# A gather, combine and scatter stage: ten groups of 500 edges in place of twenty pairs of 128

## The chip, the cores and the metric

The kernel runs on one core of a Trainium2 chip. The metric is the device time of one execution in microseconds. The engines are PE (matrix products), DVE (vector), ACT (scalar), POOL (which also issues the indirect DMAs) and SP (which issues plain DMAs); each works through its own queue in order, and they wait for one another by semaphores.

## What is computed

A graph layer with its normalizations, followed by a small mixture of experts. The change touches the graph layer's edge stage alone:

```python
x = layernorm(x)                                  # 10000 x 512
msg = relu(x[src] + edge_attr @ W_e + b_e)        # 5000 edges, 64 attributes each
aggr = segment_sum(msg, dst, num_segments=10000)  # dst is sorted, with many repeats
h = (1 + eps) * x + aggr
h = silu(batchnorm(h @ W1 + b1)); h = silu(batchnorm(h @ W2 + b2))
x = x0 + h                                        # x0 as it was; then the experts
```

## The kernel before

Four stages run one after the other, `edge_aggregate`, `gnn_up`, `gnn_down` and `mixture`; each ends when all its engines are done. Between the first two lies the table `aggregate` in the chip's memory, 10,000 rows of 512 numbers and some rows more for what is thrown away. SP fills it with zeros in pieces of 1 MB (L161), the edge stage adds the messages to it by indirect DMAs that add at the destination (`scatter`, L263), and `gnn_up` reads it.

The 5000 edges go in 20 pairs of tiles of 128 edges, the last one padded. Four sets of buffers (`PU`) are used in turn. For a pair g:

- SP (ACT for the first four) loads source and destination indices by column, the attributes, and the destinations by row, repeated over all partitions (`load`, L136, seven DMAs).
- POOL gathers 2 x 128 rows of `x` by source index into `xg` (`gather`, L248).
- DVE's `front` (L293) compares each destination with all destinations of the pair, which gives the 0/1 matrix `sel` (L304). With `before` it finds out whether an edge has an earlier one with the same destination (L309); the address `idx` of such an edge is a row that is thrown away (L319). Then the mean and the variance of each gathered row (L315 to L326).
- POOL's `root` (L257) takes the inverse root, DVE's `shift` the bias (L329).
- PE's `embed` (L367) transposes the attributes and multiplies them by `web`, in float32. ACT's `normalize` (L192) makes `xn`, DVE's `add` (L335) adds the product from PSUM, ACT takes the positive part `msg` (L212).
- PE's `combine` (L381) multiplies `msg` by `sel` in float32, so that every edge holds the sum of all edges of the pair with its destination; ACT copies that from PSUM to `comb` (L220).
- POOL scatters the 2 x 128 rows. Since two pairs can hold the same destination, each scatter waits until the one before it has landed (semaphore `sca`, L266).

The order of POOL's queue is: for each pair scatter(g), gather(g+4), root(g+3). DVE's: shift(g+1), add(g), front(g+2). ACT's: attributes(g+1), the positive part of g, normalize(g+1), the copy of g. Two turns before the end DVE also splits W1 into a high and a low part (L406 to L409), for the products of the next stage.

Of the kernel before, what the change touches and what calls it, by code (L numbers as in the profile page):

```python
# [14 lines left out]
P = 128  # L15
# [4 lines left out]
PAIRS = -(-E // (2 * P))  # L20
ER = E - (PAIRS * 2 - 1) * P
PU = 4
ROOTS = 3
ZQ = 3
TRASH = 2 * P
# [25 lines left out]
def edge_aggregate(nc, sem, psum, ident, x, src, dst, edge_attr, W_e, b_e, agg, W1, w1, vectors, vec):  # L51
# [5 lines left out]
    with ExitStack() as ctx:  # L57
        def sb(name, shape, dt=F32):
            return ctx.enter_context(nc.sbuf_tensor(name, shape, dt))

        def buffers(name, shape, dt=F32, n=PU):
            return [sb(f"{name}{i}", shape, dt) for i in range(n)]

        zeros = sb("zeros", [P, 2048])
        web = sb("web", [ED + 1, H])
        before = sb("before", [P, 2, 2 * P])
        trash = sb("trash", [P, 2])
        mhalf = sb("mhalf_e", [P, 2])
        eaT = sb("eaT", [ED + 1, PU, 2 * P])


        dcol, scol = buffers("dcol", [P, 2], I32, PU + 1), buffers("scol", [P, 2], I32, PU + 1)
        drow, ea = buffers("drow", [P, 2 * P], I32, PU + 1), buffers("ea", [P, 2, ED], F32, PU + 1)
        xg = buffers("xg", [P, 2, H])
        dcolf, cnt, away = buffers("dcolf", [P, 2]), buffers("cnt", [P, 2]), buffers("away", [P, 2])
        sel, scr = buffers("sel", [P, 2, 2 * P]), sb("scr", [P, 2, 2 * P])
        idx = buffers("idx", [P, 2], I32)
        st, mv = buffers("est", [P, 2, 6]), buffers("emv", [P, 2, 2])
        ve, rs, nb = buffers("eve", [P, 2]), buffers("ers", [P, 2]), buffers("enb", [P, 2])
        xn, pre = buffers("exn", [P, 2, H]), buffers("pre", [P, 2, H])  # L80
        msg, comb = buffers("msg", [P, 2, H]), buffers("comb", [P, 2, H])
        tp, emb, cps = psum[0:2], psum[2:6], psum[6:8]
# [3 lines left out]
        vld = sem("vectors_loaded")  # L86
        w1ld, w1h, w1l = sem("w1_loaded"), sem("w1_hi_done"), sem("w1_lo_done")
        ld = [sem(f"edge_loaded{i}") for i in range(PU + 1)]
        gat = [sem(f"rows_gathered{i}") for i in range(PU)]
        sca = sem("rows_added")  # L90
        dcf, sl, ct, aw, ix = sem("dstf"), sem("sel_ready"), sem("cnt_ready"), sem("away_ready"), sem("idx_ready")
        bst, bag, vpe, rst, nbr = sem("estats"), sem("emeanvar"), sem("evar_eps"), sem("erstd"), sem("emean_rstd")
        xnr, prr, msr = sem("exn_ready"), sem("pre_ready"), sem("msg_ready")
        tpr, etr, emr, cpr, cbr = sem("ea_transposed"), sem("eaT_ready"), sem("emb_ready"), sem("comb_psum"), sem("comb_ready")
        CONST = 10
        LOADS = 7 * 16
# [3 lines left out]
        pieces = [(c, min(c + 2048, cols)) for c in range(0, cols, 2048)]  # L100
        TURNS = PAIRS // PU

        def pair_of(it, u):

            it, u = it + u // PU, u % PU
            return it * PU + u, u, it

        def inputs(g, u):

            return PU if isinstance(g, int) and g == PAIRS - 1 else u  # L110

        def loaded(g, u, it):

            return (ld[PU], LOADS) if inputs(g, u) == PU else (ld[u], (it + 1) * LOADS)

        def turns(eng, turn):

            turn(0)
            with eng.Fori(1, TURNS - 2) as it:
                turn(it)  # L120
            turn(TURNS - 2)
            turn(TURNS - 1)

        def exists(it, u):

            return not isinstance(it, int) or it * PU + u < PAIRS

        def from_(g, least):

            return not isinstance(g, int) or g >= least  # L130

        def all_zero(eng):
            for i in range(ZQ):
                eng.wait_ge(zeroed[i], 16 * len(pieces[i::ZQ]))

        def load(eng, it, u):  # L136
            g, u, it = pair_of(it, u)
            i, e0 = inputs(g, u), g * 2 * P
            if i == u and from_(g, PU):

                wait_apart(eng, (const, CONST), (ix, 2 * (g - PU + 1)), (gat[u], it * 32), (tpr, g - PU + 1))
            rows = (P, P) if i == u else (P, ER)
            for j, p in enumerate(rows):
                span = bass.ds(e0 + j * P, p)
                eng.dma_start(scol[i][0:p, j:j + 1], src[span].rearrange("(p a) -> p a", a=1)).then_inc(ld[i], 16)
                eng.dma_start(dcol[i][0:p, j:j + 1], dst[span].rearrange("(p a) -> p a", a=1)).then_inc(ld[i], 16)
                eng.dma_start(ea[i][0:p, j, :], edge_attr[span, :]).then_inc(ld[i], 16)
            eng.dma_start(drow[i][:, 0:sum(rows)], dst[bass.ds(e0, sum(rows))].rearrange("(a p) -> a p", a=1)
                          .to_broadcast([P, sum(rows)])).then_inc(ld[i], 16)

        with nc.Block() as block:
            @block.sync
            def _(sp):
                sp.dma_start(web[0:ED, :], W_e).then_inc(wld, 16)
                sp.dma_start(web[ED:ED + 1, :], b_e.rearrange("(a n) -> a n", a=1)).then_inc(wld, 16)

                sp.wait_ge(const, 1)
                for i, (c0, c1) in enumerate(pieces):
                    if i >= ZQ:
# [1369 lines left out]
```

## Time and profile before

| | us |
|---|---|
| three runs, median (lowest to highest) | 2173.71 (2170.03 to 2175.91) |
| the profiled execution | 2172.88 |
| its span | 2171.1 |
| edge stage, first instruction to the next stage's first load | 2.2 to 242.4 |

| engine | busy us of the span | share |
|---|---|---|
| PE | 1948.6 | 90% |
| DVE | 1212.7 | 56% |
| ACT | 1005.5 | 46% |
| POOL | 387.8 | 18% |

A share of the whole span is a mean over four stages; for the edge stage one reads the views cut to its stretch of time. Timelines give an operation's start and length, and in brackets how long its engine had nothing to do before it, and what ended that.

### The profile page before, as it was taken

The numbers are of one execution on the slowest core, as the hardware profiler recorded it, in microseconds if no ns is written. First come the engines' busy times: TensorE is split into PE (matmuls) and PEld (weight loads), VectorE is DVE, ScalarE is ACT, GpSimd is POOL, SyncE is SP. The second block draws the span as 40 slices with busy tenths as digits, with TensorE's granted clock in tenths as the row PEclk, the third lists the DMA queues.
The fourth block names the chain that finished last, engine by engine and source line by source line (L and its number), as shares of the span: only waits on it lengthen the run. The fifth ranks groups of instructions, "written<-read, shape, count | busy, mean of one in ns | idle before, by whom it ended". The sixth has DMA issues, their size and how long they took to land. (4 is left out here: it accounts for less than half of the span.)

```text
span 2171.1 us, 42529 instructions
## 1 busy us (share of the span) xinstructions
PE 1948.6 (90%) x15080; PEld 1395.1 (64%) x15080; DVE 1212.7 (56%) x2533; ACT 1005.5 (46%) x1742; POOL 387.8 (18%) x481
## 2 busy tenths in 40 slices
PE   0777399999999799999999589999899999999997
PEld 0233278888888588888887466656666666666653
DVE  1457356566566343434342667667576676767654
ACT  0445123333233375656563455546464554655542
POOL 1576230000000000000000422212121221222200
PEclk9999699999999899999999799999999999999999
DMA  9886746566656443434341744334343333434311
GB/s 379 205 153 122 161 132 184 158 180 182 166 169 171 151 152 118 165 118 165 117 166 56 242 152 137 105 103 131 95 128 99 127 112 100 136 104 137 99 55 64
DMA packets 182828, 309.29 MB, mean 142 GB/s; under 512 B 33065, under 2 KB 107305, under 8 KB 179594
## 3 DMA queue, kind: packets, MB, share of 16 engines
q1 hardware_dynamic: 169674, 285.35, 42.0%
q0 software_dynamic: 8960, 20.98, 5.1%
q8 instruction: 103, 1.69, 0.3%
q10 hardware_dynamic: 4032, 0.80, 0.2%
q14 instruction: 59, 0.48, 0.1%
HBM read 172.20 MB, written 134.87 MB: 141 GB/s over the span
## 5 line engine op out<-in xcount | busy, mean ns | idle before, releaser
L1397 PE MATMUL bank<-f2s,inner_bd 128*32 128x512 f32 x2560 | 304.8, 606 | 1.5 <-issue 1.2
L1301 ACT ACTIVATE inter_hi<-bank 128x512 fp32r<-128x512 f32 x320 | 191.2, 598 | 200.3 <-PE bank L1397 199.4
L1232 DVE TENSOR_TENSOR inter_lo<-bank,inter_hi 128x512 fp32r<-128x512 f32 x320 | 220.1, 689 | 95.7 <-ACT inter_hi L1301 95.0
L419 PE MATMUL bank<-ahi,w_hi 128*128 128x500 f32 x640 | 250.8, 392 | 14.4 <-DVE alo L760 14.4
L606 ACT ACTIVATE h1o<-bank,b_by_channel 128x500 f32<-128x500 f32 x160 | 108.5, 678 | 327.4 <-PE bank L421 327.4
L419 PE MATMUL bank<-hhi,w_hi 128*128 128x500 f32 x640 | 251.6, 393 | 2.5 <-DVE hlo L567 2.5
L421 PE MATMUL bank<-hhi,w_lo 128*128 128x500 f32 x640 | 249.8, 390 | 0.0
L420 PE MATMUL bank<-hlo,w_hi 128*128 128x500 f32 x640 | 249.4, 390 | 0.0
L420 PE MATMUL bank<-alo,w_hi 128*128 128x500 f32 x640 | 249.2, 389 | 0.0
L421 PE MATMUL bank<-ahi,w_lo 128*128 128x500 f32 x640 | 248.9, 389 | 0.0
L1281 ACT ACTIVATE yT<-bank 128x512 f32<-128x512 f32 x320 | 173.6, 597 | 83.8 <-PE bank L1371 83.2
L573 DVE BATCH_NORM_STATS2 stats<-h1o 128x500 f32 (+1 forms) x160 | 103.6, 676 | 163.0 <-ACT h1o L606 163.0
L1397 PEld LDWEIGHTS bank<-f2s,inner_bd 128*32 128x32 f32 x2560 | 74.1, 111 | 148.0 <-issue 145.5
L760 DVE TENSOR_TENSOR alo<-a_whole,ahi 128x500 fp32r<-128x500 f32 x160 | 108.7, 679 | 106.3 <-ACT ahi L796 106.3
L766 DVE BATCH_NORM_STATS2 stats<-h2o 128x500 f32 (+1 forms) x80 | 52.6, 677 | 175.5 <-ACT h2o L804 175.5
L419 PEld LDWEIGHTS bank<-ahi,w_hi 128*128 128x128 f32 x640 | 120.6, 189 | 42.1 <-DVE alo L760 17.8
L1370 PE MATMUL bank<-perm_bd,xn_hi 128*128 128x512 f32 x320 | 140.9, 440 | 2.2 <-ACT yT L1281 2.2
L419 PEld LDWEIGHTS bank<-hhi,w_hi 128*128 128x128 f32 x640 | 120.7, 189 | 26.8 <-DVE hlo L567 2.9
L1406 PE MATMUL bank<-inter_hi,back_bd 128*128 128x512 f32 x320 | 128.1, 400 | 10.2 <-DVE back_bd L1224 10.2
L421 PEld LDWEIGHTS bank<-hhi,w_lo 128*128 128x128 f32 x640 | 120.9, 189 | 24.9
L421 PEld LDWEIGHTS bank<-ahi,w_lo 128*128 128x128 f32 x640 | 120.7, 189 | 25.1
L420 PEld LDWEIGHTS bank<-hlo,w_hi 128*128 128x128 f32 x640 | 120.9, 189 | 24.6
(124 smaller groups left out, 3287.1 us busy)
## 6 DMA issues: line engine op xcount, KB each, us to landing
h1T<-h1o SPq DMA_DIRECT2D x19, 2000.0 KB, 8.1
h1in<-h1T SPq DMA_DIRECT2D x19, 2000.0 KB, 9.6
aggregate<-zeros SPq DMA_DIRECT2D x20, 1024.0 KB, 8.3
h2in<-h2T SPq DMA_DIRECT2D x40, 512.0 KB, 4.0
x<-in_x SPq DMA_DIRECT2D x80, 256.0 KB, 2.6
x<-x SPq DMA_DIRECT2D x80, 256.0 KB, 3.8
x_back<-x SPq DMA_DIRECT2D x80, 256.0 KB, 3.8
out<-x_back SPq DMA_DIRECT2D x80, 256.0 KB, 2.0
```

The costliest lines, as they stand in the source:

```text
L419: nc.tensor.matmul(out, w_hi[:, k, cols], a_hi[:, k, :], start=(k == 0), stop=False)
L420: nc.tensor.matmul(out, w_hi[:, k, cols], a_lo[:, k, :], start=False, stop=False)
L421: last = nc.tensor.matmul(out, w_lo[:, k, cols], a_hi[:, k, :], start=False, stop=(k == chunks - 1))
L573: nc.vector.bn_stats(stats1[:, m, bass.ds(c * 6, 6)], h1o[b][:, m, :]).then_inc(str_, 1)
L606: nc.scalar.activation(h1o[b][:, m, :], mb[m % 4][:, 0:CW], ACT.Identity, bias=b1c[:, m:m + 1]).then_inc(evr, 1)
L760: nc.vector.tensor_tensor(alo[b][:, k, :], aw[:, k, :], ahi[b][:, k, :].bitcast(F32), ALU.subtract).then_inc(lor, 1)
L1232: nc.vector.tensor_tensor(ilo[u % QB][:, :], bI[u % QB][:, :], ihi[u % QB][:, :].bitcast(F32), ALU.subtract).then_inc(ilr, 1)
L1281: nc.scalar.activation(yT[:, c, :, j * GB:(j + 1) * GB], bD[c % 2][:, :].rearrange("p (e g) -> p e g", g=GB), ACT.Copy).then_inc(yr, 1)
L1301: nc.scalar.activation(ihi[n % QB][:, :], bI[n % QB][:, :], ACT.Copy).then_inc(ihr, 1)
L1370: nc.tensor.matmul(o, xhi[j % 2][:, c * P:(c + 1) * P], r, start=True, stop=False)
L1397: last = nc.tensor.matmul(bI[b][32 * i:32 * i + 32, :], ibd[:, e, j, :, :].rearrange("p s g -> p (s g)"), f2s[:, e, :], start=True, stop=True)
L1406: nc.tensor.matmul(bA[:, :], rbd[:, b, :], ihi[b][:, :], start=(b == 0), stop=False)
```

## The change

The edges go in ten windows of four tiles of 125 edges. Edge number p x 40 + t stands in row p of tile t, so that one DMA loads all source indices, one all destinations and two all attributes, ahead of the zeros. Gathers and scatters still move 128 rows per tile; the last three are padding (source 0, destination a row that is thrown away, three rows of zeros in `comb`).

- Destinations by row come from PE (`spread`: a transpose of the repeated column, into one bank of PSUM), no longer from a DMA. DVE compares straight from that bank.
- A window's tiles share destinations, so tile j of a window sums over tiles j to 3 of it: ten products with a `sel` of 125 x 125. They are made twice, for a high and a low part of the message, in float32r (`mhi`, `mlo`, which lie in the buffers of W2).
- ACT's `normalize` is gone. DVE makes x times the inverse deviation plus the embedding in one instruction, ACT adds the bias with the positive part, and copies that to the high part; DVE subtracts it for the low part.
- Four windows of gathered rows (`XW`) are kept, two windows of `comb`.
- W1 and the vectors are loaded after the zeros. W1 is split at the end of DVE's queue.
- All loops are written out, with no loop in the hardware.

In the diff below the bodies of `matches`, `statistics` and `attributes`, the declarations and the constants' set-up are left out.

```diff
-PAIRS = -(-E // (2 * P))
-PU = 4
-ROOTS = 3
-TRASH = 2 * P
+EP, ET = 125, 40
+EW = 4
+EN = ET // EW
+XW = 4
+TRASH = EW * P
...
@@ SP @@
+                sp.dma_start(scol[0:EP, :], src.rearrange("(p i) -> p i", i=ET)).then_inc(lds, 16)
+                sp.dma_start(dcol[0:EP, :], dst.rearrange("(p i) -> p i", i=ET)).then_inc(ldd, 16)
+                attr = edge_attr.rearrange("(p i) d -> p i d", i=ET)
+                for p0, p1 in ((0, EP // 16 * 16), (EP // 16 * 16, EP)):
+                    sp.dma_start(ea[p0:p1, :, :], attr[p0:p1]).then_inc(lde, 16)
...
@@ ACT @@
+                def messages(w):
+
+                    for t in window(w):
+                        s = slot(t)
+                        act.wait_ge(prr, t + 1)
+                        nc.scalar.activation(xg[0:EP, s, :], xg[0:EP, s, :], ACT.Relu, bias=nb[0:EP, t:t + 1]).then_inc(msr, 1)
+                        act.wait_ge(msr, t + 1)
+                        if w >= 2:
+                            act.wait_ge(cpr, EW * (w - 1))
+                        nc.scalar.activation(mhi[0:EP, t % (2 * EW), :], xg[0:EP, s, :], ACT.Copy).then_inc(mhr, 1)
+
+                def collect(w):
+
+                    if w >= 2:
+                        act.wait_ge(sca, 16 * EW * (w - 1))
+                    for t in window(w):
+                        act.wait_ge(cpr, t + 1)
+                        nc.scalar.activation(comb[0:EP, t % (2 * EW), :], cps[t % 3][0:EP, :], ACT.Copy).then_inc(cbr, 1)
+
+                for w in range(EN):
+                    if w + 1 < EN:
+                        attributes(w + 1)
+                    messages(w)
+                    if w >= 1:
+                        collect(w - 1)
+                collect(EN - 1)
...
@@ POOL @@
+                def gather(w):
+                    if w >= XW:
+
+                        pool.wait_ge(mhr, EW * (w - XW + 1))
+                        pool.wait_ge(mlr, EW * (w - XW + 1))
+                    for t in window(w):
                         nc.gpsimd.indirect_dma_start(
+                            out=xg[:, slot(t), :], out_offset=None, in_=x, in_offset=bass.IndirectOffsetOnAxis(
+                                ap=scol[:, t:t + 1], axis=0)).then_inc(gat[w % XW], 16)
+                def scatter(w):
+
+                    pool.wait_ge(ix, w + 1)
+                    if w >= 1:
+                        pool.wait_ge(sca, 16 * EW * w)
+                    for t in window(w):
+                        pool.wait_ge(cbr, t + 1)
                         nc.gpsimd.indirect_dma_start(
...
+                for w in range(XW):
+                    gather(w)
+                for w in range(XW - 1):
+                    root(w)
+                for i in range(ZQ):
+                    pool.wait_ge(zeroed[i], 16 * len(pieces[i::ZQ]))
+                for w in range(EN):
+                    scatter(w)
+                    if w + XW < EN:
+                        gather(w + XW)
+                    if w + XW - 1 < EN:
+                        root(w + XW - 1)
...
@@ DVE @@
+                def combine(w):
+
+                    a, b = w * EW, (w + 1) * EW
+                    dve.wait_ge(rst, w + 1)
+                    nc.vector.scalar_tensor_tensor(out=nb[0:EP, a:b], in0=mv[0:EP, a:b, 0], scalar=-1.0, in1=rs[0:EP, a:b],
...
+                    for t in window(w):
+                        dve.wait_ge(emr, t + 1)
+                        nc.vector.scalar_tensor_tensor(out=xg[0:EP, slot(t), :], in0=xg[0:EP, slot(t), :],
+                                                       scalar=rs[0:EP, t:t + 1], in1=emb[t % 2][0:EP, :],
+                                                       op0=ALU.mult, op1=ALU.add).then_inc(prr, 1)
+                    if w >= 2:
+                        dve.wait_ge(cpr, EW * (w - 1))
+                    for t in window(w):
+                        dve.wait_ge(mhr, t + 1)
+                        nc.vector.tensor_tensor(mlo[0:EP, t % (2 * EW), :], xg[0:EP, slot(t), :],
+                                                mhi[0:EP, t % (2 * EW), :].bitcast(F32), ALU.subtract).then_inc(mlr, 1)
+
+                matches(0)
+                statistics(0)
+                statistics(1)
+                for w in range(EN):
+                    if w + 1 < EN:
+                        matches(w + 1)
+                    if w + 2 < EN:
+                        statistics(w + 2)
+                    combine(w)
+                dve.wait_ge(w1ld, 16)
+                for k in range(KH):
+                    split_weight(nc.vector, w1["whole"], w1["hi"], w1["lo"], w1h, w1l, k)
...
@@ PE @@
+                def embed(w):
+                    pe.wait_ge(etr, w + 1)
+                    for t in window(w):
+                        j = t % EW
+                        if t >= 2:
+                            pe.wait_ge(prr, t - 1)
+                        nc.tensor.matmul(emb[t % 2][0:EP, :], eaT[:, w % 2, j * EP:(j + 1) * EP], web[:, :],
                                          start=True, stop=True).then_inc(emr, 1)
...
+                def add_up(w):
+                    pe.wait_ge(mlr, EW * (w + 1))
+                    for t in window(w):
+                        j = t % EW
+                        if t >= 3:
+                            pe.wait_ge(cbr, t - 2)
+                        for i in range(j, EW):
+                            s = (w % 2) * EW + i
+                            pick = sel[w % 3][i][0:EP, j * EP:(j + 1) * EP]
+                            nc.tensor.matmul(cps[t % 3][0:EP, :], pick, mhi[0:EP, s, :], start=(i == j), stop=False)
+                            last = nc.tensor.matmul(cps[t % 3][0:EP, :], pick, mlo[0:EP, s, :], start=False,
+                                                    stop=(i == EW - 1))
...
+                for w in range(EN):
+                    if w + 1 < EN:
+                        spread(w + 1)
+                        turn(w + 1)
+                    embed(w)
+                    if w >= 1:
+                        add_up(w - 1)
+                add_up(EN - 1)
```

`matches(w)` compares tile i with tiles 0 to i of its window (125 to 500 columns), finds earlier edges of the same destination with `before`, and makes `idx`; it waits for `spread(w)`, which in turn waits until the comparisons of the window before have read the bank. `statistics(w)` waits for all four gathers of the window. `turn` transposes the attributes.

## Rows read from the trace of the kernel before

**Rows 1.** Busy time by stage: span, busy us (instructions) by engine, clock, DMA share, GB/s.
```profile
68.00:236.00 168.00, 120.60 (x257) 48.15 (x255) 89.91 (x315) 74.33 (x128) 111.84 (x89) 0.89 0.76 141
```

**Rows 2.** Waits, 60 to 240 us: who waited for whom, total us, times, longest.
```profile
POOL aggregate L269 <- DMA aggregate<-comb,idx: 31.4, 14, 5.8
```

**Rows 3.** Timeline of POOL: start us, us, operation, [idle before <- what ended it].
```profile
115.37 1.64 POOL L269 DMA_INDIRECT aggregate<-comb,idx  x1 [1.22 <-DMA aggregate<-comb,idx]
...
117.31 1.57 POOL L269 DMA_INDIRECT aggregate<-comb,idx  x1 [0.30 <-ACT exn L199]
...
119.19 1.02 POOL L253 DMA_INDIRECT xg<-in_x,scol  x1 [0.30 <-issue]
...
120.52 0.98 POOL L253 DMA_INDIRECT xg<-in_x,scol  x1 [0.30 <-issue]
...
123.22 1.64 POOL L269 DMA_INDIRECT aggregate<-comb,idx  x1 [0.97 <-ACT comb L220]
```

**Rows 4.** DVE's groups up to 240 us (busy, mean ns), and its timeline from 249.
```profile
L343 DVE TENSOR_TENSOR pre<-exn,bank 128x512 f32<-128x512 f32 x40 | 25.8, 684 | 2.4 <-ACT exn L199 1.9
...
L309 DVE CUSTOM_DVE_ANT_0 scr<-sel,before 128x256 f32<-128x256 f32 x40 | 15.2, 416 | 0.0
...
L409 DVE TENSOR_TENSOR w_lo<-weight_whole,w_hi 128x1024 fp32r<-128x1024 f32 x4 | 4.9, 1226 | 0.1
...
249.46 2.47 DVE L543 BATCH_NORM_STATS2 st<-xt 125x6 f32<-125x512 f32 x4 [6.84 <-DMA xt<-in_x]
...
252.26 0.17 DVE L548 TENSOR_SCALAR ve<-mv 125x4 f32<-125x4 f32 x1
```

**Rows 5.** ACT's groups up to 240 us: busy us, mean ns, idle before.
```profile
L212 ACT ACTIVATE msg<-pre 128x512 f32<-128x512 f32 x40 | 24.1, 627 | 36.7 <-DVE pre L343 36.7
...
L220 ACT ACTIVATE comb<-bank 128x512 f32<-128x512 f32 x40 | 23.9, 597 | 56.0 <-PE bank L388 41.7 <-issue 9.6 <-DMA aggregate<-comb,idx 4.7
```

**Rows 6.** Timeline of PE and its weight loads, three stretches.
```profile
201.23 0.50 PEld L388 LDWEIGHTS bank<-msg,sel 128*128 128x128 f32 x2 [6.24 <-ACT msg L212]
...
204.80 0.34 PEld L388 LDWEIGHTS bank<-msg,sel 128*128 128x128 f32 x1 [0.52 <-issue]
...
205.49 0.19 PEld L388 LDWEIGHTS bank<-msg,sel 128*128 128x128 f32 x1 [0.35 <-issue]
...
207.88 1.98 PE L378 MATMUL bank<-web,eaT 65*128 65x512 f32 x4 [0.73 <-ACT eaT L190]
...
268.95 0.39 PE L419 MATMUL bank<-hhi,w_hi 128*128 128x500 f32 x1
...
269.18 0.39 PE L420 MATMUL bank<-hlo,w_hi 128*128 128x500 f32 x1
```

**Rows 7.** Timeline of POOL and SP's queue at the end of the edge stage.
```profile
223.85 1.54 POOL L269 DMA_INDIRECT aggregate<-comb,idx  x1 [4.20 <-DMA aggregate<-comb,idx]
...
231.68 1.55 POOL L269 DMA_INDIRECT aggregate<-comb,idx  x1 [4.44 <-DMA aggregate<-comb,idx]
...
233.53 1.56 POOL L269 DMA_INDIRECT aggregate<-comb,idx  x1 [0.30 <-issue]
...
242.44 0.85 SPq L482 DMA_DIRECT2D xt<-in_x  x2
```

**Rows 8.** Timeline of POOL and DVE, 112 to 119 us: a gather and its statistics.
```profile
112.41 0.98 POOL L253 DMA_INDIRECT xg<-in_x,scol  x1 [0.30 <-issue]
...
118.27 1.29 DVE L315 BATCH_NORM_STATS2 est<-xg 128x6 f32<-128x512 f32 x2 [0.91 <-DMA xg<-in_x,scol]
```

**Rows 9.** First scatter; DMA from 24 to 28 us: packets, MB, share of engines.
```profile
67.81 1.65 POOL L269 DMA_INDIRECT aggregate<-comb,idx  x1 [1.42 <-ACT comb L220]
...
DMA packets 504, 1.66 MB, mean 416 GB/s; under 512 B 257, under 2 KB 257, under 8 KB 346
...
q0 software_dynamic: 121, 0.36, 22.6%
```

**Rows 10.** Busy time by stage, columns as in rows 1, while two scatters drain.
```profile
226.00:228.00 2.00, 0.00 (x0) 0.00 (x0) 0.00 (x0) 0.00 (x0) 1.24 (x1) 1.00 0.95 125
```

More of the change, by code:

```diff
@@ L59, in sb @@
             return ctx.enter_context(nc.sbuf_tensor(name, shape, dt))
-        def buffers(name, shape, dt=F32, n=PU):
-            return [sb(f"{name}{i}", shape, dt) for i in range(n)]
-        zeros = sb("zeros", [P, 2048])
+        zeros = sb("zeros", [P, ZC])
         web = sb("web", [ED + 1, H])
[L66 to L72, printed above, removed]
@@ L132, in all_zero @@
[L132 to L149, printed above, removed]
+        pieces = [(c, min(c + ZC, cols)) for c in range(0, cols, ZC)]
@@ L177, in _ @@
-                turns(sp, turn)
+                for i in range(ZQ):
+                    sp.wait_ge(zeroed[i], 16 * len(pieces[i::ZQ]))
+                sp.dma_start(w1["whole"][:, :, :], W1.rearrange("(k p) n -> p k n", p=P)).then_inc(w1ld, 16)
+                with nc.allow_non_contiguous_dma(reason="vectors by channel"):
+                    for name in ("b1", "g1", "beta1", "b2", "g2", "beta2"):
+                        sp.dma_start(vec[name][:, :], vectors[name].rearrange("(m p) -> p m", p=P)).then_inc(vld, 16)
@@ L222, in _, with attributes @@
-                for u in range(PU):
-                    load(act, 0, u)
-                act.wait_ge(const, CONST)
-                attributes(0, 0)
-                normalize(0, 0)
-                turns(act, turn)
+                def attributes(w):
+                    act.wait_ge(tpr, w + 1)
+                    if w >= 2:
+                        act.wait_ge(emr, EW * (w - 1))
+                    nc.scalar.activation(eaT[0:ED, w % 2, :], tp[w % 2][0:ED, 0:EW * EP], ACT.Copy).then_inc(etr, 1)
@@ L346, in turn @@
-                def turn(it):
-                    for u in range(PU):
-                        if exists(it, u + 1):
-                            shift(it, u + 1)
-                        add(it, u)
-                        if exists(it, u + 2):
-                            front(it, u + 2)
-                    if isinstance(it, int) and it == TURNS - 2:
-                        dve.wait_ge(w1ld, 16)
-                        for k in range(KH):
-                            split_weight(nc.vector, w1["whole"], w1["hi"], w1["lo"], w1h, w1l, k)
@@ L392, in turn @@
-                def turn(it):
-                    for u in range(PU):
-                        if exists(it, u + 1):
-                            embed(it, u + 1)
-                        combine(it, u)
+                def turn(w):
+                    if w >= 2:
+                        pe.wait_ge(etr, w - 1)
+                    for t in window(w):
+                        j = t % EW
+                        last = nc.tensor.transpose(tp[w % 2][0:ED, j * EP:(j + 1) * EP], ea[:, t, :], ident[0:EP, 0:EP])
+                    last.then_inc(tpr, 1)
```

309 lines of the change are left out of this document (107 added, 202 removed).

## The prediction

> **What bounds the kernel now.** I read the busy table by stages first. The edge stage ends where the sync engine issues the next stage's loads, at 242.4 us of a 2171.1 us span [rows 7]. From 68 to 236 us, the part in which rows are scattered, no engine is full: PE 121 of 168 us, DVE 90, ACT 74, and POOL 112 [rows 1]. So a chain through several engines sets the pace, and the waits and the order of POOL's work tell which. POOL waited 31.4 us, 14 times, for the previous pair's scatter to land [rows 2]. Its timeline shows a period: two scatters, two gathers, one root, then a short wait (0.97 us after the root in the one shown); from 115.37 to 123.22 us that is 7.85 us, of which scatters cost 1.94 us each from start to start and gathers 1.33 [rows 3]. Twenty pairs are paced by POOL's issues and by the scatter landings together. Before the first scatter, at 67.81 us [rows 9], the stage waits for the fill of `aggregate` with zeros. Only the edge stage is changed, so what I forecast is its end, shifted; everything after 242.4 us is taken to shift with it.
>
> **What the change does to that loop.** The number of indirect DMAs stays at 40 gathers and 40 scatters of 128 rows, so POOL's issue time stays too. What goes are nineteen landing waits, which become nine, and the small loads for each pair. What is new is a ring. POOL's queue holds scatter(w), then gather(w+4), then root(w+3). ACT's holds messages(w+1) ahead of collect(w), so scatter(w) cannot begin before combine(w+1) is over on DVE. And DVE's queue holds statistics(w+4) ahead of combine(w+2). Hence combine(w+2) waits for statistics(w+4), that for gather(w+4), that for POOL to have issued scatter(w), and that for combine(w+1): each window goes once round the whole ring, with POOL's 4 scatters and 4 gathers inside it. Four buffers of gathered rows don't help, since the statistics run two windows ahead of the combination and the scatter one behind. In the kernel before the statistics for pair g+4 stand ahead of the addition for pair g+3 while scatter(g) follows the addition for pair g: three pairs of slack instead of one window.
>
> **The ring's parts**, from the start c of combine(w+1):
> - *c to the first collected tile: 7.4 us (6.5 to 8.4).* DVE's combining instruction takes about 0.68 us per tile by its nearest relative, the addition from PSUM [rows 4]. ACT then does two passes per tile, each about 0.63 us [rows 5]: 4 x 1.28 us with 0.02 us for the wait between them, starting at c + 0.77, ends at c + 5.9. The collection, 0.60 us [rows 5], ends at 6.5. That holds if PE keeps up. PE must first run two embeddings that wait for the first two combinings (only two banks), then 8 products for the first tile. At the full clock (2.4 GHz) an embedding takes 2 x 0.43 us (four records in 1.98 us) and a product 0.23 us [rows 6], ready at c + 0.8 + 1.7 + 1.8 = 4.3, hidden behind ACT. At half clock (1.2 GHz) both double: c + 0.8 + 3.4 + 3.6 = 7.8, and 8.4 collected. After a wait of 6.24 us the same weight load took 0.34 us until 204.80 and 0.19 from 205.49, so PE ran slow for 4.3 us [rows 6]. In the new ring PE waits longer than that each time, so I take a value between: 7.4.
> - *Four scatters: 7.6 us (7.2 to 7.8).* 1.94 us start to start [rows 3], and 1.85 where DVE is idle [rows 7]. The landing of the window before is long over.
> - *Four gathers: 5.0 us (4.9 to 5.3).* 3 x 1.33 + 0.98 [rows 3].
> - *Landing of the last gather: 3.0 us (0 to 4.9).* One wait of DVE shows it: the second gather of a pair is issued from 112.41 to 113.39, and its statistics start at 118.27, 4.9 us later, 0.91 of them DVE's wait for that DMA [rows 8]. That gather shared the DMA engines with the small loads, which are gone; it stood behind two scatters in the same queue, and now behind four, which landed meanwhile. I take 3.0, nearer the row than nothing.
> - *Statistics: 3.0 us* by the same four-tile sequence in the next stage, 249.46 to 252.43 [rows 4], and 0.2 us for the shift ahead of the first combining.
>
> Sum 7.4 + 7.6 + 5.0 + 3.0 + 3.2 = **26.2 us per window** (all low ends 21.8, all high ends 29.6), against two of the old periods, 15.7. Six windows go round the ring (gathers 4 to 9, combine 2 to 7).
>
> The Trainium skill ("DMA: Bandwidth & Descriptors", section "Anatomy of one DMA") gives a DMA issued by GpSimd about 2.0 us plus its bytes at 436 GB/s: 2.6 us for 256 KB, where the one landing that this case's trace shows took 4.9, so the two don't agree. By the page, an estimate, the ring would be 25.8 us and the end 6 x 0.4 = 2.4 us earlier.
>
> **The start.** All 16 first gathers (4.2 MB) and the edge attributes (1.3 MB, now one load) share the DMA engines with the fill: 10,512 rows of 2 KB, 21.5 MB. In all that is 27.2 MB with the weights, at 416 GB/s [rows 9] 65 us. Beginning at 3.5 to 5 us the fill is over near 69 us. During the fill gathers got 22.6% of the engines [rows 9], 0.36 MB in 4 us; at that rate 4.2 MB take 47 us from 7 us on, with more queued perhaps 35. So window 3 is there at 42 to 55 us and combine(1), which also has to follow combine(0) by a DVE turn of some 16 us, starts at 53 to 65. The first scatter then starts at **71 us** (68 to 80), against 67.81 before [rows 9].
>
> **The middle.** combine(2) starts 7.6 + 5.0 + 3.0 + 3.2 = 18.8 us after the first scatter, and I add 1.5 us for the load of W1 and the short vectors, which now run there: 91.3. Five more turns: combine(7) starts at 91.3 + 131 = **222.3**.
>
> **The end.** No gathers are left. DVE then goes at its own pace: combine 7 to 8 us, a wait for PE's row transposes behind the sums of the window before, the matches. The matches are two passes over 125 + 250 + 375 + 500 = 1250 columns, at 0.416 us per 256 [rows 4] 2.0 us each. combine(8) starts at about +15 and combine(9) at +24. Scatter(7) starts at +22. From there the scatters are a chain again, since scatter(w+1) waits for scatter(w) to land. DMA engines are 95% busy while two scatters drain and no other traffic runs [rows 10], and two scatters take 7.83 us from first issue to the next pair's issue [rows 7]. With the second issue 1.9 later, each costs the engines about 2.1, so a window takes 7.83 + 2 x 2.1 = 12 us. Scatter(9) starts at +46. The last pair before took from 231.68 to 242.44 [rows 7], 10.8 us with the end of the stage; four scatters take 4.2 more: +61. The stage ends at 222.3 + 61 = 283, against 242.4: **+40 us**.
>
> What is moved out of the loop costs nothing that I can see. The split of W1 goes to the end of DVE's queue: eight instructions of at most 1.23 us [rows 4], 9.8 us, beside the last two windows' scatters, over 25 us; without that cover it would cost its 9.8. W1's load now follows the fill in SP's queue, 200 us ahead of its use. The extra transposes, the low part's subtraction and the products in two parts are on PE and DVE inside the 12 us that the ring leaves them free; were there no ring they would bound it, below. The waits that DVE now makes for the row transposes hold up the statistics queued behind, but those wait for gathers anyway.
>
> Against the profiled execution's 2172.9 us (2171.1 of it span), 0.8 below the median of the three runs, 2173.7, the forecast is 2172.9 + 40 = **2213 us**.
>
> **Rivals.**
> 1. *Faster: the gathers don't end the wait.* If each window's gathers landed before DVE had done its matches, the pace would be DVE's with PE's: matches 4.7, statistics 3.0, combine 7.0, and 1.6 of waiting for PE, 16.3 us. combine(9) would start at 63 + 8 x 16.3 = 193, the last scatter 10 us later, and the stage would end at 193 + 10 + 15 = 218, so 24 us earlier: 2149. It decides where first tile, scatters, gathers and landing together (23.0) fall under DVE's 16.3 less 3.2. Half the landing waits and no small loads speak for it; that each of POOL's issues has its own 1 to 1.7 us in the timeline [rows 3], in the queue's order, speaks against. Chance 0.09, and 0.03 for something between that comes out within 0.3% of now.
>  The same section of the Trainium skill calls descriptor generation small, with many descriptors before it shows. By that the 12.6 us of issues would shrink to the engines' time, some 8.4 us for scatters and 2 for gathers, the ring to about 24 and the time to 2200, inside my range; POOL's rows speak against it, and I give it no more than 0.05 of the forecast's chance.
> 2. *Slower still: the start.* If 16 gathers queued during the fill hold up both more than in proportion, or the vectors' short loads collide with the first scatters, the first scatter comes at 85: 2227. Together with a ring at its upper end, 29.6, 2247. For it: gathers got 22.6% of the engines only. Chance 0.14.
> 3. *The edit doesn't do what it says*, if PE is at half clock throughout and the split products cost double: the ring goes to 28 and the time to 2224; that lies in my range.
>
> **How the numbers follow.** Forecast 0.74, start or ring at the upper end 0.14, faster 0.09, no change 0.03. The ring's parts will hardly all lie at one end; with 22.5 and a first scatter at 68 the time is 2188, with 29 and a first scatter at 80 it is 2240. This holds nearly all of the first case and half the second. Faster by over 0.3% (6.5 us; about what a measurement of this kernel can tell) 0.09, within 0.03, slower 0.88.
>
> **What would show it.** Right: between about 80 and 220 us the timeline of POOL shows four scatters, four gathers, a root and then idle time of some 12 us until ACT's collected tile; DVE's statistics wait for the gathered rows about six times, for some 5 to 10 us each; combine starts 26 us apart; PE's clock falls in each gap. Wrong: scatters start 16 us apart with no such waits (rival 1), or the first scatter is past 80 us (rival 2). If the ring is right but the time is off by over 15 us, the landing of the gathers and the start are the terms that I know least.

## The result and the profile after

The changed kernel takes 2241.34 us (2237.31 to 2244.55, four runs), beside 2171.87 (2168.82 to 2175.91) of the kernel before on the same chip: a ratio of 1.0318 (1.0303 to 1.0333). Slower was forecast, at 2213 us; the time lies 28 us above that and one above the top of the range.

The profiled execution took 2240.54 us, 2238.3 of them span. Cut by the first loads of each stage in SP's queue, the two traces stand so (us):

| | edge stage ends | `gnn_up` | `gnn_down` | `mixture`, to the end |
|---|---|---|---|---|
| before | 242.44 | 500.6 | 453.1 | 974.9 |
| after | 295.10 | 503.0 | 451.9 | 988.3 |
| difference | +52.7 | +2.4 | -1.2 | +13.4 |

So the edge stage lost more than the 40 us forecast, and 13.4 us were lost in the last stage, of whose code the diff touches nothing.

Busy time of the changed kernel from 70 to 210 us (columns as in rows 1). PE's clock is 0.60 there; [rows 1] had 0.89.

```profile
70.00:210.00 140.00, 55.88 (x149) 34.28 (x150) 54.33 (x147) 36.30 (x58) 56.76 (x45) 0.60 0.48 94
```

No engine is busy even half the time, less than before: a chain sets the pace. The waits from 70 to 245 us (who waited for whom: total us, times, longest):

```profile
POOL aggregate L210 <- ACT comb L158: 89.1, 10, 16.8
DVE est L266 <- DMA xg<-in_x,scol: 66.0, 6, 20.9
```

In [rows 2] POOL waited for the landing of the scatter before; now it waits for ACT's collected tiles, and DVE six times for gathered rows. One turn in POOL's timeline, which answers to [rows 3]:

```profile
187.07 1.64 POOL L210 DMA_INDIRECT aggregate<-comb,idx  x1 [14.29 <-ACT comb L158]
189.02 1.57 POOL L210 DMA_INDIRECT aggregate<-comb,idx  x1 [0.30 <-issue]
190.90 1.59 POOL L210 DMA_INDIRECT aggregate<-comb,idx  x1 [0.30 <-issue]
192.79 1.55 POOL L210 DMA_INDIRECT aggregate<-comb,idx  x1 [0.30 <-issue]
194.64 1.02 POOL L194 DMA_INDIRECT xg<-in_x,scol  x1 [0.30 <-issue]
195.97 0.98 POOL L194 DMA_INDIRECT xg<-in_x,scol  x1 [0.30 <-issue]
197.26 0.95 POOL L194 DMA_INDIRECT xg<-in_x,scol  x1 [0.30 <-issue]
198.51 0.95 POOL L194 DMA_INDIRECT xg<-in_x,scol  x1 [0.30 <-issue]
199.48 1.05 POOL L201 TENSOR_TENSOR ers<-eve,mhalf_e 125x4 f32<-125x4 f32 x1
```

Four scatters, four gathers, a root, then 14 us of nothing. The other engines in the same turn (timelines of DVE, PE and ACT, rows left out):

```profile
177.54 1.41 DVE L282 SCALAR_TENSOR_TENSOR xg<-xg,ers,bank 125x512 f32<-125x512 f32 x2
...
178.34 3.78 PE L331 MATMUL bank<-web,eaT 65*125 65x512 f32 x4 [14.86 <-DVE xg L282]
...
184.90 0.63 PE L344 MATMUL bank<-w_lo,sel 125*125 125x512 f32 x1
185.33 0.54 PE L343 MATMUL bank<-w_hi,sel 125*125 125x512 f32 x1
...
185.63 0.60 ACT L158 ACTIVATE comb<-bank 125x512 f32<-125x512 f32 x1 [1.31 <-PE bank L344]
...
202.16 2.47 DVE L266 BATCH_NORM_STATS2 est<-xg 125x6 f32<-125x512 f32 x4 [9.18 <-DMA xg<-in_x,scol]
...
205.21 1.41 DVE L282 SCALAR_TENSOR_TENSOR xg<-xg,ers,bank 125x512 f32<-125x512 f32 x2
```

From combine to combine that is 205.21 - 177.54 = 27.67 us. PE's clock while the first tile's products run, and just after (busy time, the clock is the third number from the end):

```profile
178.30:185.30 7.00, 6.96 (x12) 4.12 (x13) 4.54 (x7) 5.30 (x8) 0.00 (x0) 0.50 0.00 0
186.00:188.00 2.00, 2.00 (x10) 1.61 (x9) 0.00 (x0) 0.83 (x2) 0.93 (x1) 1.00 0.00 0
```

After 14.86 us without work PE is at the lower level (1.2 GHz) for these 7 us, and at 2.4 GHz in the two us just after. The first scatter and the end of the stage, which answer to [rows 9] and [rows 7] (timelines of POOL and of SP's queue; the second row is the next stage's first load):

```profile
73.33 1.66 POOL L210 DMA_INDIRECT aggregate<-comb,idx  x1 [32.20 <-issue]
...
295.10 0.86 SPq L442 DMA_DIRECT2D xt<-in_x  x2
```

### The profile page after: what moved, and what is told of

Read it like the earlier page. It is cut to its first block and busy times, and to the rows that moved or that the text cites. A ratio compares the mean times of both kernels' runs of the same rounds, so it can differ in the third digit from the quotient of the medians.

```text
span 2238.3 us, 42019 instructions
## 1 busy us (share of the span) xinstructions
PE 1940.9 (87%) x15160; PEld 1420.0 (63%) x15160; DVE 1241.5 (55%) x2506; ACT 1005.0 (45%) x1732; POOL 375.3 (17%) x469
## 5 line engine op out<-in xcount | busy, mean ns | idle before, releaser
L331 PE MATMUL bank<-web,eaT 65*125 65x512 f32 x80 | 56.9, 849 | 132.8 <-DVE xg L282 132.7
```

## Experiments

Two questions were open: is the ring the cause in the edge stage, and which of its terms were wrong; and where do the 13.4 us of the last stage come from. Single executions stand beside one profiled execution of the changed kernel, 2240.5 us.

### The ring, cut at three places

*Statistics one window ahead of the combination instead of two* (DVE's queue alone):

```diff
-                statistics(1)
...
-                    if w + 2 < EN:
-                        statistics(w + 2)
+                        statistics(w + 1)
```

> The changed kernel with DVE's statistics one window ahead of the combination in place of two, and nothing else: the gathers of window w+4 then have two windows' time. Ring theory: the ring opens, scatters of one window after the other start 16 to 20 us apart in place of 27.6, no waits of 9 us of the statistics for gathers, and the edge stage ends at 73 + 9 x 17.5 + 15 = 246 (235 to 270) in place of 295. Rival 'work': PE at half clock and DVE's own work set the 27.6, so it stays within 2 of that and the end at 295.

Measured: 2180.52 us (2177.43 to 2183.84), ratio to the kernel before 1.0033 (1.0018 to 1.0047); the edge stage ends at 234.7. First scatters come about 18 us apart (121.72, 140.39, 158.07), and from 70 to 245 us DVE waits for gathered rows once, 10.9 us, instead of six times, 66.0. What ends its waits instead is, most often, PE's bank of row transposes (timeline of DVE):

```profile
142.15 1.89 DVE L246 TENSOR_SCALAR sel<-bank,dcolf 125x125 fp32r<-125x125 f32 x4 [3.32 <-PE bank L319]
146.18 2.46 DVE L266 BATCH_NORM_STATS2 est<-xg 125x6 f32<-125x512 f32 x4
149.22 1.41 DVE L282 SCALAR_TENSOR_TENSOR xg<-xg,ers,bank 125x512 f32<-125x512 f32 x2
```

The statistics follow the matches with no wait for a DMA. Moving one call in one queue takes 60 us off the edge stage: looking further ahead was what cost. Without the ring the kernel is still only level with the one before.

*POOL's gather(w+4) ahead of scatter(w)*, the wait for the zeros ahead of the first scatter alone:

```diff
-                for i in range(ZQ):
-                    pool.wait_ge(zeroed[i], 16 * len(pieces[i::ZQ]))
                 for w in range(EN):
-                    scatter(w)
                     if w + XW < EN:
                         gather(w + XW)
+                    if w == 0:
+                        for i in range(ZQ):
+                            pool.wait_ge(zeroed[i], 16 * len(pieces[i::ZQ]))
+                    scatter(w)
```

> The changed kernel with one change of order on POOL: gather(w+4) stands ahead of scatter(w), and the wait for the zeros ahead of scatter(0) alone. The gathers then leave the ring by another door than in the run with the statistics nearer: combine(w+2) waits for gathers that stand behind scatter(w-1), two windows' time. Ring theory: scatters of successive windows 17 to 19 us apart, at the pace of DVE with PE, and an edge stage that ends at 73 + 9 x 17.8 + 15 = 248 (232 to 260). Rival 'DVE's order' (it was the statistics' place as such, with their work ahead of the combination, that cost the time): 27 apart, end near 290.

Measured: 2179.35 us, one run; the edge stage ends at 234.0, 14 us earlier than worked out but inside the bounds. The period is about 18 us from the third window on (18.9 from 124.15 to 143.02), and DVE waits for gathered rows once, 5.6 us.

*PE sums window w-1 ahead of the embedding of w, and ACT collects it ahead of the messages of w*:

```diff
@@ PE @@
-                    embed(w)
                     if w >= 1:
                         add_up(w - 1)
+                    embed(w)
@@ ACT @@
-                    messages(w)
                     if w >= 1:
                         collect(w - 1)
+                    messages(w)
```

> The changed kernel with PE's sums of window w-1 ahead of the embeddings of window w, and ACT's collection of w-1 ahead of the messages of w; DVE and POOL as in the changed kernel. Scatter(w) then follows combine(w), not combine(w+1). Ring theory: a turn of the ring spans two windows: combine(w) to the first scatter 12 us, scatters 7.6, gathers 4.8, landing 2.7, statistics 3.2, together 30.3 for two, so 15 to 16 us per window and an edge stage that ends at 73 + 9 x 15.5 + 15 = 228 (220 to 245). Rival 'work': 27 per window, end 290.

Measured: 2169.05 us, one run; the edge stage ends at 227.9, as expected, with the last stage as slow as in the changed kernel (986.1). A period is 14 to 20 us, 15.5 in the mean of all nine. POOL's idle time before the first scatter of a window, 14.29 us in the changed kernel, is now long and short in turn, 6.27 us at most while there are gathers left; two successive windows (timeline of POOL):

```profile
138.16 1.64 POOL L210 DMA_INDIRECT aggregate<-comb,idx  x1 [3.77 <-ACT comb L158]
...
152.51 1.65 POOL L210 DMA_INDIRECT aggregate<-comb,idx  x1 [0.60 <-issue]
```

Three edits, in DVE's queue, in POOL's, and in PE's with ACT's, bring the stage from 295 to between 228 and 235. The first two break a link of the ring; the third stretches a turn of it over two windows. That shows the ring. The pace that is left, about 18 us in the first two and 15.5 in the third, lies on either side of rival 1's 16.3; what sets it in each was not tested.

### The size of the ring: PE's speed

*High parts only.* The products of the low part are left out, so the sums lack it: ten products fewer per window on PE, the rest in the same order.

```diff
-                            nc.tensor.matmul(cps[t % 3][0:EP, :], pick, mhi[0:EP, s, :], start=(i == j), stop=False)
-                            last = nc.tensor.matmul(cps[t % 3][0:EP, :], pick, mlo[0:EP, s, :], start=False,
+                            last = nc.tensor.matmul(cps[t % 3][0:EP, :], pick, mhi[0:EP, s, :], start=(i == j),
                                                     stop=(i == EW - 1))
```

> The changed kernel without the products of the low part: 10 in place of 20 for each window, so the sums have the high part alone. It asks what PE's slow products are worth in the ring. First tile: four products at 0.43 us fewer, 1.7 us, of which ACT's messages (done 6.8 us after the first combining) take back 0.5: ring 26.4 in place of 27.6, edge stage ends near 286 (283 to 289). If PE's products were not in the ring: 295 within 1.5. PE's program is some 200 instructions shorter, so the last stage may take another time than 988.

Measured: 2213.71 us, one run; the edge stage ends at 287.8, first scatters 26.5 us apart in the mean of five turns in place of 27.7. Four products fewer ahead of the first tile, at 0.43 us each at half clock, are 1.7 us; 1.2 a turn came, what was expected with the 0.5 that ACT's messages take back. So PE's products are on the ring. (The last stage, 969.9 us, changes with PE's program; see below.)

*PE kept busy while it waits.* 128 transposes of the identity, into a bank that is free, in each of windows 2 to 7:

```diff
                     for t in window(w):
                         j = t % EW
+                        if j == 2 and 2 <= w <= 7:
+                            for _ in range(128):
+                                nc.tensor.transpose(tp[w % 2][0:P, 0:P], ident[:, :], ident[:, :])
                         if t >= 2:
                             pe.wait_ge(prr, t - 1)
```

> The changed kernel, where PE transposes the identity 128 times into a free bank in each of windows 2 to 7, while it waits for the combining; the ring and the outputs stay. Theory A (the granted clock, which falls while PE waits, made the first tile late: PE took 7.0 us from its first embedding to the first tile's last product where 4.3 had been assumed): PE needs about 3.5 to 4.5 us there, ACT sets the first tile at about 6.6 us after the combining begins instead of 8.7, the first scatters come about 25.6 apart instead of 27.7, and the edge stage ends at 280 to 285 instead of 295. Rival B (the time goes into waits between engines, not into PE's speed): the distance stays at 27 to 28 and the end at 293 to 297. The last stage is not part of this test, since PE's code moves.

Measured: 2230.04 us, one run; first scatters 25.4 to 27.0 us apart (26.0 in the mean of the five turns from 103.09 to 233.18, where the changed kernel has 27.7), and the edge stage ends at 286.5, 8.6 us earlier, though not at the 280 to 285 expected. The turn that begins at 172.81 (busy time and PE's clock from its first embedding on; then rows of ACT's and POOL's timelines):

```profile
173.60:178.60 5.00, 4.99 (x18) 3.40 (x19) 3.99 (x6) 4.87 (x8) 0.00 (x0) 1.00 0.00 0
```

```profile
178.72 2.19 ACT L158 ACTIVATE comb<-bank 125x512 f32<-125x512 f32 x4
...
180.14 1.64 POOL L210 DMA_INDIRECT aggregate<-comb,idx  x1 [11.99 <-ACT comb L158]
```

At full clock ACT collects from 178.72, 5.9 us after the combining began, where the changed kernel collects 8.1 us after it, and the scatter starts after 7.3 us and not 9.5. The gain is not the same in every turn, since the transposes don't last as long as PE's wait. In two turns PE had 1.06 and 1.03 us without work behind them and stayed at full clock. In three it had 2.58, 2.40 and 2.23 us; it then began at full clock and fell to half in the middle of its burst, and the scatter started after 7.8 us (timeline of PE, one of the three; a product is 0.40 us long at full clock):

```profile
147.82 2.31 PE L334 MATMUL bank<-web,eaT 65*125 65x512 f32 x4 [2.58 <-DVE xg L282]
...
150.37 0.63 PE L347 MATMUL bank<-w_lo,sel 125*125 125x512 f32 x1
```

In the first turn, with 11.62 us behind the transposes, PE was at half clock from its start, and nothing was gained. So the lower clock costs about 2.2 us of a turn, and theory A holds for the size of a turn. That only two of six turns were kept at full clock explains part of why the end is later than expected; in the longest turn (27.0) the last gather also landed 3.9 us after its issue in place of 2.7, for which the run shows no cause.

### The last stage

Its PE program runs as a loop in the hardware. In the kernel before, PE waits 4.09 us for nothing that the profile shows ("issue") at one product of a turn of that loop, then runs on for 11 us, and has one gap of 1.19 us behind that. In the changed kernel the same product waits as long, and two shorter gaps follow within those 11 us (timelines of PE, first before, then after):

```profile
1448.65 0.42 PE L1353 MATMUL bank<-eye,perm_new 128*128 128x64 f32 x1 [4.09 <-issue]
1449.00 3.64 PE L1424 MATMUL bank<-yT,f1s 128*32 128x64 f32 x128
```

```profile
1500.54 0.42 PE L1313 MATMUL bank<-eye,perm_new 128*128 128x64 f32 x1 [4.15 <-issue]
1500.88 0.64 PE L1384 MATMUL bank<-yT,f1s 128*32 128x64 f32 x10
1503.51 3.26 PE L1384 MATMUL bank<-yT,f1s 128*32 128x64 f32 x115 [1.99 <-issue]
...
1511.28 0.31 PE L1384 MATMUL bank<-yT,f1s 128*32 128x64 f32 x6 [1.10 <-issue]
```

All its loops being written out, the new edge stage has another number of PE instructions ahead of that loop. So the place of the loop in PE's program was one theory; another was that the rows added to `aggregate` (`TRASH`) move the tables that the last stage reads; a third was an after-effect of the longer edge stage. The same pad at the head of PE's queue was put into both kernels, and the rows into the kernel before:

```diff
+                for _ in range(16):
+                    nc.tensor.transpose(tp[0][0:P, 0:P], ident[:, :], ident[:, :])
```

> The changed kernel with 16 transposes of the identity into a free bank at the start of PE's queue in the edge stage, where PE has nothing to do: 32 more instructions in PE's program, everything behind them stands 32 later. Nothing else differs. The last stage took 988.3 us in the changed kernel and 974.9 before, with unchanged code. Theory 'place of PE's code': the gaps of about 2 us after each turn of PE's loop there come from where the loop's first instruction stands, so the last stage changes by more than 5 us, to somewhere between 970 and 985; the edge stage still ends near 295. Theory 'table addresses' (aggregate has 256 rows more, so all later tables lie elsewhere) and theory 'after-effect of the longer edge stage': the last stage stays at 988 within 3.

> The kernel before with the same 16 transposes at the start of PE's queue. Theory 'place of PE's code': the last stage may move by several us, in either direction, from 974.9; the edge stage still ends near 242. Theories 'table addresses' and 'after-effect': it stays at 975 within 3 and the time at 2172 within 5.

```diff
-TRASH = 2 * P
+TRASH = 4 * P
```

> The kernel before with 512 rows for what is thrown away in place of 256, as the changed kernel has it; every later table lies 512 KB further and the fill is 0.5 MB longer (1.2 us). Theory 'table addresses': the last stage takes about 988 and the whole some 2186. Theories 'place of PE's code' and 'after-effect': the last stage stays at 975 within 3, the whole at 2173 within 5.

Two other lengths of the pad in the changed kernel, 6 and 64 transposes:

> The changed kernel with 6 transposes of the identity (12 PE instructions) at the head of PE's queue in place of the 16 tried before. Theory (the last stage's time hangs on where the branch back of PE's innermost loop and its target lie in the program): the last stage is 966 to 989 us, and whichever it is, PE's idle gaps put down to issue at the innermost loop move with it, near 29 us for the upper end and near 16 for the lower. Rival (the 16 transposes helped by something else that they do early in the edge stage, so fewer help in proportion): the last stage comes out near 980.

> The changed kernel with 64 transposes of the identity (128 PE instructions) at the head of PE's queue. Theory (place of the code): the last stage is either near 966 or near 988, with the issue gaps at PE's innermost loop to match, and not below 960. Rival (the transposes help by themselves): the last stage is clearly below the 966.5 us of the 16 transposes, near 940 or less, or unchanged from that.

Measured, with all of PE's waits that the trace puts down to issue from 1150 to 2300 us (the time is the median of the runs, the rest is read from the profiled execution; the last five rows are the runs of the ring):

| | time, us | edge end | last stage | PE's issue waits |
|---|---|---|---|---|
| before | 2171.87 | 242.4 | 974.9 | 37.9 |
| before, 16 transposes | 2171.71 | 241.4 | 973.9 | 37.7 |
| before, `TRASH` doubled | 2174.27 | 245.1 | 971.8 | 35.4 |
| after | 2241.34 | 295.1 | 988.3 | 51.0 |
| after, 6 | 2243.70 | 295.2 | 991.7 | 51.1 |
| after, 16 | 2217.66 | 292.3 | 966.5 | 34.4 |
| after, 64 | 2227.02 | 293.6 | 976.8 | 41.2 |
| after, statistics later | 2180.52 | 234.7 | 988.5 | 49.0 |
| after, gather first | 2179.35 | 234.0 | 991.2 | 52.1 |
| after, sums first | 2169.05 | 227.9 | 986.1 | 51.6 |
| after, high parts only | 2213.71 | 287.8 | 969.9 | 38.5 |
| after, PE kept busy | 2230.04 | 286.5 | 989.5 | 52.5 |

The runs of the ring are further witnesses. The first three of them keep the number of PE's instructions: with an edge stage 60 us shorter, their last stage is that of the changed kernel, within 3 us, which is also about how far such a time repeats. So the theory of an after-effect falls. High parts only has 200 PE instructions fewer. The waits of PE that carry most of the sums for the changed kernel, then with 16, then with 64 transposes (columns as above):

```profile
PE bank L1384 <- issue: 29.2, 23, 3.0
PE bank L1313 <- issue: 19.9, 5, 4.5
```

```profile
PE bank L1315 <- issue: 17.9, 5, 3.7
PE bank L1386 <- issue: 15.9, 18, 2.5
```

```profile
PE bank L1315 <- issue: 23.5, 5, 5.6
PE bank L1386 <- issue: 16.8, 20, 4.5
```

Against the kernel before, the ratios are 1.0204 (1.0178 to 1.0231) with 16 transposes, and 0.9989 (0.9976 to 1.0001) and 0.9998 (0.9983 to 1.0013) for the pad and the rows in the kernel before. So the rows in `aggregate` do nothing, and the theory of the tables falls. The pad in the kernel before moved its last stage by 1.0 us only, so it speaks neither for nor against the place. In the changed kernel it does: that 32 instructions at the start of the program, 1250 us before, take 21.8 us off the last stage (to 966.5, where 970 to 985 was expected), that 12 take nothing off, where help in proportion would have given 980, and 128 less than 32, shows that what counts is how far they move the program, not the work that they do. The granted clock of the last stage is 0.96 to 0.98 in all these runs. PE's issue waits carry most of the differences: 16.6 of the 21.8 us with 16, 9.8 of 11.5 with 64, and 13.1 of the 13.4 between the two kernels. "Either near 966 or near 988" was a miss: with 64 the inner loop's gaps fell as expected (16.8), but those at L1315 grew from 19.9 to 23.5, and the stage came out between.

What fills these gaps the traces don't show. The Trainium skill ("Runtime: NRT & Kernel Launch", section "Instruction fetch mechanics") says that an engine's instructions are fetched in blocks of 256 and that a taken branch out of the blocks at hand stalls until its target is fetched; a gap of about 4 us that comes once a turn, and others whose size moves with the loop's place, agree with that. So does the run in which PE is kept busy: its program is 1536 instructions longer, six times 256, and its last stage is that of the changed kernel, 989.5 us. But it was not made to test this, and no run here measured a fetch.

### Both orders together

The first and the third edit above, with 16 transposes at the head of PE's queue:

> The changed kernel with the statistics one window ahead, the sums and the collection ahead of the next window's embeddings and messages, and the 16 transposes at the start of PE's queue. Ring theory: no ring left; POOL's own 13.5 us per window or DVE's 14 to 15.5 set the pace, the edge stage ends at 73 + 9 x 14.5 + 15 = 218 (210 to 232). With the last stage at 966.5 as with the 16 transposes alone, the whole takes 218 + 502 + 452 + 967 + 2 = 2141 (2130 to 2160). Theory 'place of PE's code' is wrong if the last stage is back at 988.

Measured: 2133.62 us (2130.61 to 2137.35), ratio to the kernel before 0.9823 (0.9806 to 0.9839), the fastest of all. The edge stage ends at 209.85, a shade under the lowest time expected, and the last stage takes 965.5 us, as expected. Now POOL goes from window to window with no wait, 14.1 us each (its timeline):

```profile
142.70 1.25 POOL L201 TENSOR_TENSOR ers<-eve,mhalf_e 125x4 f32<-125x4 f32 x1
144.15 1.67 POOL L210 DMA_INDIRECT aggregate<-comb,idx  x1 [0.20 <-issue]
...
156.87 1.20 POOL L201 TENSOR_TENSOR ers<-eve,mhalf_e 125x4 f32<-125x4 f32 x1
158.27 1.67 POOL L210 DMA_INDIRECT aggregate<-comb,idx  x1 [0.20 <-issue]
```

Its scatter follows its root with 0.20 us between. So the groups of 500 edges, in this order, take 14.1 us for four tiles where two of the old pairs take 15.7; the order in which three queues take their work had hidden it. Of the 42.7 us between its profiled execution and the one before, 32.6 are the edge stage's, and 9.4 the last stage's, whose work is the same. The pad alone gives the kernel before nothing (2171.71).

## Why the prediction was right, and where it was wrong

**Right: the ring.** The forecast read off the queues that each window would go once round all of it, and the trace shows the order, the six waits of DVE, the 14 us of idle time on POOL (12 forecast) and the falling clock. Cutting it at either of two links, or stretching it over two windows, ends that pace.

**Its terms**, in the turn shown, beside the forecast:

| | forecast | measured | from |
|---|---|---|---|
| combine to the first scatter | 7.4 (6.5 to 8.4) | 9.53 | 177.54 to 187.07 |
| four scatters | 7.6 | 7.57 | to 194.64 |
| four gathers | 5.0 | 4.82 | to 198.51 + 0.95 |
| landing of the last | 3.0 (0 to 4.9) | 2.70 | to 202.16 |
| statistics and shift | 3.2 | 3.05 | to 205.21 |
| sum | 26.2 | 27.67 | |

Only the first was mis-sized, and beyond its upper end. Two things went into it. The value between full and half clock, 7.4, was taken from a stretch with 4.3 us of slow PE after a wait of 6.24 [rows 6]; after 14.86 PE was slow for 7.0, so that the first tile was collected at 8.69, even behind the 8.4 given for half clock. The run with transposes shows the end that was given for full clock, ACT's 6.5, to be right: 5.9 + 0.6. The other 0.84 us are between ACT's last collected element (185.63 + 0.60) and POOL's first scatter, a step that the sum didn't have; it is 0.84 or 0.85 us in each of the six turns. Rival 3, a ring of 28 us by half clock, came nearest to what happened, although PE is slow only for the first 7 us of a turn: the first tile's products lie just there.

The Trainium skill ("DMA: Bandwidth & Descriptors", "Anatomy of one DMA") gave 2.6 us for the landing as an estimate; the 2.70 measured agrees, counted like the forecast's term from the end of POOL's instruction (from its start it is 3.65). The 4.9 of [rows 8] had other loads beside it. That section's small cost of descriptors does not agree with POOL: an issue still takes 1.25 to 1.95 us from start to start.

**The start** was 2.3 us late: the first scatter at 73.33 against 71, set by the fill: combine(1) began at 54.83, inside the 53 to 65 forecast, and the load that SP issues behind the fill came at 72.51. The first turn took 30.2 us, where 27.7 had been worked out, with the loads of W1 and the vectors in SP's queue from 72.51 to 90; the 1.5 us given for them were too few. The excess is the landing: it took 5.35 us in this turn (85.67 to 91.02) and 2.5 to 2.8 in the other five, and only here small packets of the plain queue, 4304 of them, took 44.8% of the DMA engines' time beside it.

**The end** was right: 295.10 less 242.12, the first scatter of window 6, is 53.0 us; 53.3 had been worked out (283 less 229.7). Splitting W1 ended at 272 us beside the last scatters, hidden as supposed.

So the edge stage's 12.7 us beyond the forecast are 2.3 at the start, 2.5 in the first turn, 7.6 in the five turns after it (138.6 us against 131), less 0.3 at the end, and 0.6 that was rounded off between 283 and 242.4 + 40.

**Wrong: "everything after 242.4 us is taken to shift with it".** This step failed. The later stages took 14.6 us longer, 13.4 in the last, though not a line of it changed. Without that the profiled execution would have taken 2240.5 - 14.6 = 2225.9 us, inside the range; with the pad, which changes no work of any stage, the kernel takes 2217.66. The forecast had a term for every queue and none for where the program's later part would come to lie. It was one of two misses of like size: without the edge stage's 12.7 us the time would have been 2227.8, also inside. Both had to come together for the 1.3 us by which the time lies above the range, less than its four runs differ.

**What was not expected at all** is how little stood between this change and a gain. The forecast named the two orders that make the ring but gave a ring-free pace only as a rival, for a case in which the gathers land in time. In the experiments one moved call brought a pace near it (18 us) and the time of the kernel before; the second reordering, with the pad, brought the gain.

## What to carry to other kernels

When work is regrouped into larger windows, follow one window's buffer through every queue: if what an engine does ahead for window w+2 stands before what window w needs to free its buffer, that order sets the pace, and moving one call one window back helps. More buffers were not tried. A term that has an engine start after a long wait is priced by a row in which it waited as long, and each hop from engine to engine gets its own price. A change that alters the number of PE instructions ahead of a loop in the hardware can move that loop's time by a per cent with nothing changed in it; compare with the same kernel padded by a few instructions before a stage is blamed.

## What the runs showed of the hardware

- After 14.86 us without work PE ran 7.0 us at the 1.2 GHz level (granted clock 0.50 from 178.3 to 185.3), then at 2.4 GHz (1.00 from 186 to 188); with transposes until 1.03 us before, it was 1.00 from the first product. With transposes until 2.58 us before, it was 1.00 for the first embeddings and 0.50 from 150.0 to 152.4.
- 32 PE instructions more at the head of the program made a loop 1250 us later 21.8 us shorter, 128 more 11.5 shorter, 12 more 3.4 longer, which is not clear of how far it repeats (986.1 to 991.2 with the number unchanged); in the other kernel 32 more changed 1.0 us. PE's gaps without a cause in the profile went from 51.0 to 34.4 us in the first case.
- From the end of ACT's copy to the start of the scatter that POOL issues on it lie 0.84 or 0.85 us in six turns.
- A gather of 128 rows of 2 KB landed 2.5 to 2.8 us after POOL had issued it, in five turns with only the kernel's own scatters and gathers beside it. With small loads beside it, it was 5.35 us, and 4.9 in [rows 8].
